# Epsilon added by GpSimd, indices and places without conversions, and a new order of VectorE's small steps

## What is computed

```
x = x + attn_a(layernorm(x));  x = x + ffn(layernorm(x))
x = x + attn_b(layernorm(x));  x = x + ffn(layernorm(x))

layernorm(x) = (x - mean) / sqrt(var + 1e-5)
ffn:  logits = tgt @ Wr.T + br;  top_v, top_i = top_k(logits, 2);  top_w = softmax(top_v)
      each token goes through its two experts (128 -> 512 relu -> 128), weighted by top_w,
      then gamma * layernorm(tgt + tgt2) + beta
```

## Time and profile before

| what | value |
|---|---|
| median of 3 runs | 945.51 us (942.33 to 946.16) |
| the profiled execution, its own time | 949.54 us |
| its span in the profile | 947.7 us |
| TensorE matmuls busy | 791.4 us, 84% |
| VectorE busy | 630.8 us, 67% |
| ScalarE busy | 473.8 us, 50% |
| GpSimd busy | 434.3 us, 46% |
| second attention, roughly | 427 to 749 us |

### The profile page before, as it was taken

How to read it: one execution, slowest core, us unless ns; L and a number is a source line. 1 busy time by engine, 2 the same in 40 slices (tenths; PEclk the granted TensorE clock), 3 DMA queues, 4 the chain that set the end, 5 groups by cost and what they waited for, 6 DMA issues and landing times.

```text
span 947.7 us, 20829 instructions
## 1 busy us (share of the span) xinstructions
PE 791.4 (84%) x6270; PEld 565.3 (60%) x6270; DVE 630.8 (67%) x2348; ACT 473.8 (50%) x1130; POOL 434.3 (46%) x516
## 2 busy tenths in 40 slices
PE   3599989988898899934899998999998799999920
PEld 1356655655687799931455555555544488999920
DVE  3457777764466466644888997898895475666657
ACT  3356666654332233312377776776766432433424
POOL 3002444443466376541243664565322475666643
PEclk9999999996799999975699998999998899999965
DMA  7635554450567777723434534443420378777754
GB/s 198 142 88 122 133 125 121 121 120 28 159 203 222 210 228 240 224 78 105 129 109 132 142 104 123 122 131 108 132 88 27 119 213 251 236 225 240 223 161 123
DMA packets 111668, 142.28 MB, mean 150 GB/s; under 512 B 14912, under 2 KB 90560, under 8 KB 108992
## 3 DMA queue, kind: packets, MB, share of 16 engines
q1 hardware_dynamic: 102480, 122.19, 47.2%
q0 software_dynamic: 9088, 18.89, 5.9%
HBM read 102.89 MB, written 36.66 MB: 147 GB/s over the span
## 4 chain that ended last, share of the span: by engine, by line
PE 55%; DVE 18%; issue 7%; DMA 7%; SPq 5%; ACT 5%; POOL 2%; DVEq 0%; POOLq 0%; ACTq 0%
PE attn L1466 13%; PE attn L740 6%; PE score L1457 6%; PE max L1457 6%; DVE mx L989 6%; PE max L706 5%; PE score L682 4%; PE misc L776 3%; PE misc L748 3%; DMA qst<-scr 2%; PE misc L806 2%; ACT prob L459 2%; PE attn L1446 2%; DMA qst<-mparts 2%; DVE stats L350 1%
## 5 line engine op out<-in xcount | busy, mean ns | idle before, releaser
L989 DVE TENSOR_REDUCE mx<-max 128x2 f32<-128x512 f32 x352 | 237.6, 682 | 83.9 <-PE max L706 77.8
L459 ACT ACTIVATE prob<-score 128x512 f32<-128x512 f32 x352 | 206.1, 602 | 118.0 <-PE score L682 115.3
L1542 POOL DMA_INDIRECT ys<-yt,idw x156 | 150.3, 964 | 113.3 <-DVE yt L1517 85.0
L1289 POOL DMA_INDIRECT xs<-row,index x128 | 127.7, 998 | 149.6 <-ACT prob L459 132.9
L1466 PE MATMUL attn<-wsl,prob 128*128 128x128 f32 x1248 | 157.4, 279 | 2.8 <-DVE prob L1530 2.1
L706 PE MATMUL max<-kst,qst 72*128 72x256 bf16 (+2 forms) x768 | 141.8, 275 | 20.1 <-DVE mx L989 13.3
L1466 PEld LDWEIGHTS attn<-wsl,prob 128*128 128x128 f32 x1248 | 149.0, 195 | 5.7 <-DVE prob L1530 3.7
L682 PE MATMUL score<-qst,kst 74*128 74x256 bf16 (+2 forms) x768 | 138.4, 270 | 3.7 <-DMA qst<-mparts 1.7
L1482 ACT ACTIVATE prob<-score,wsl 128x256 f32<-128x256 f32 x78 | 36.9, 473 | 189.8 <-PE score L1457 189.6
L740 PE MATMUL attn<-prob,vaug 128*32 128x256 f32 (+1 forms) x1536 | 119.8, 385 | 1.0 <-ACT prob L459 0.6
L368 POOL TENSOR_TENSOR rstd<-rstd,halfm 128x2 f32<-128x2 f32 (+1 forms) x65 | 51.5, 793 | 144.6 <-DVE rstd L361 143.6
(11 more groups left out here) (147 smaller groups left out, 1159.2 us busy)
## 6 DMA issues: line engine op xcount, KB each, us to landing
wsl<-in_wall SPq DMA_DIRECT2D x78, 578.0 KB, 4.3
scr<-parts SPq DMA_DIRECT2D x32, 384.0 KB, 3.0
qst<-scr SPq DMA_DIRECT2D x64, 192.0 KB
xt<-xs SPq DMA_DIRECT2D x78, 132.0 KB
kst<-scr SPq DMA_DIRECT2D x16, 576.0 KB
row<-row SPq DMA_DIRECT2D x32, 128.0 KB, 3.9
yg<-ys SPq DMA_DIRECT2D x32, 128.0 KB, 2.9
kst<-scr SPq DMA_DIRECT2D x16, 192.0 KB
```

Source lines behind the costliest of these rows:

```text
L459: nc.scalar.activation(prob[:, g % 2, k, :], pS[(g * NB + k) % 2][:, :], ACT.Exp)\
L989: nc.vector.tensor_reduce(mx[:, sl[4], a:a + 2 * n - 1:2], pM[(g * NB + k) % 2][:, :].rearrange("p (h w) -> p h w", h=n), axis=AX.X, op=AL ...
L1289: nc.gpsimd.indirect_dma_start(out=xs, out_offset=bass.IndirectOffsetOnAxis(ap=index[:, slot, c, k:k + 1], axis=0), in_=row[:, slot, c, k, ...
L1542: nc.gpsimd.indirect_dma_start(out=ys, out_offset=bass.IndirectOffsetOnAxis(ap=idw[:, k, c, 0:1].bitcast(U32), axis=0), in_=yt[:, k, c, :] ...
```

## The change

GpSimd adds epsilon itself, ahead of the power; `dve_eps` is gone. The one-hot compares the uint32 indices with the numbers of the experts directly. The sum over experts becomes a maximum (all terms but one are zero, and none is negative) and writes uint32. So `ixf` and `placed` with their conversions are gone, `choose` has five parts in place of six and `send_to` four in place of five. With the parts left, the order of `step` on VectorE is written anew: in the second attention the t norm's statistics, its mean and variance, the places and its bias stand one to two banks later than before. The final norm of the last stage keeps its epsilon on VectorE.

```diff
--- before.py
+++ after.py
@@ -209,12 +209,10 @@
         lg = sb("lg", [P, RING, QC, E])
         mx8 = sb("mx8", [P, RING, QC, 8])
         ix8 = sb("ix8", [P, RING, QC, 8], U32)
-        ixf = sb("ixf", [P, QC, 2])
         oh = sb("oh", [P, QC, 2, E])
         ohb = sb("ohb", [P, RING, QC, E], BF16)
         place = sb("place", [P, QC, E])
         pick = sb("pick", [P, QC, 2, E])
-        placed = sb("placed", [P, QC, 2])
         index = sb("index", [P, RING, QC, 2], U32)
         run = sb("run", [P, E])
         dv = sb("dv", [P, RING, 3, QC])
@@ -271,12 +269,12 @@
             return sems[name]
 
         for name in """consts_in x_in proj_in weights_in consts_made geo_made filled vaug_zero wq_ps wq_made ones_set spare_in
-            c_sum c_add c_stats1 c_stats c_eps c_rstd c_bias c_norm c_gam c_bet c_x
+            c_add c_norm c_gam c_bet c_x
             n_stats1 n_stats n_eps n_rstd n_bias ln_ready lnT_ps lnT_sb qk_ps part1 less1 part2 less2 part3 v_ps v_sb
             max_ps max_read mxT_ps m_hi m_lo exp_ps exp_done av_done o_sb oT_ps rden_done on_done onT_ps onT_sb
             pr_ps x_ready t_stats1 t_stats t_eps t_rstd t_bias t_ready tT_ps tT_sb lg_ps lg_done mx8_done ix8_done
-            ixf_done diff e_done oh_done ohb_done den_done w0_done w1_done rank_ps place_done rank_read pick_done
-            placed_done index_done id_done chain chosen_made table_ps tiles_known pad_known pads_in xT_ps xT_sb idw_done h_ps h_act h_dve y_ps
+            diff e_done oh_done ohb_done den_done w0_done w1_done rank_ps place_done rank_read pick_done
+            index_done id_done chain chosen_made table_ps tiles_known pad_known pads_in xT_ps xT_sb idw_done h_ps h_act h_dve y_ps
             ysum_sb xf_done yt_sb out_w flags_set x_bet l_add l_stats1 l_stats l_eps l_rstd l_bias l_norm l_gam
             l_x""".split():
             s_(name)
@@ -355,14 +353,11 @@
                 ins = nc.vector.bn_aggr(mv[:, which, slot, c, :], stats[:, which, c, :])
             return ins
 
-        def dve_eps(dve, which, pre, v, slot):
-
-            dve.wait_ge(pre + "_stats", v)
-            nc.vector.tensor_scalar(rstd[:, which, slot, :, 0], mv[:, which, slot, :, 1], EPS, None, ALU.add)\
+        def pool_rstd(pool, which, pre, v, slot):
+
+            pool.wait_ge(pre + "_stats", v, apart=True)
+            nc.gpsimd.tensor_scalar(rstd[:, which, slot, :, 0], mv[:, which, slot, :, 1], EPS, None, ALU.add)\
                 .then_inc(s_(pre + "_eps"), 1)
-
-        def pool_rstd(pool, which, pre, v, slot):
-
             pool.wait_ge(pre + "_eps", v)
             half = halfm[:, which, :] if isinstance(which, slice) else halfm[:, 0, :]
             nc.gpsimd.tensor_tensor(rstd[:, which, slot, :, 1], rstd[:, which, slot, :, 0], half, ALU.pow)\
@@ -1016,8 +1011,6 @@
                         for w in range(which.start, which.stop):
                             ins = dve_mean_var(w, slot)
                         ins.then_inc(s_("n_stats"), 1)
-                    elif i == 2:
-                        dve_eps(dve, which, "n", v, slot)
                     elif NORM in on_:
                         dve_bias(dve, LN, "n", v, slot)
 
@@ -1063,10 +1056,8 @@
                                                 ALU.subtract).then_inc(s_("diff"), 1)
                     elif i == 3:
                         dve.wait_ge("ix8_done", v)
-                        nc.vector.tensor_copy(ixf[:, :, :], ix8[:, slot, :, 0:2]).then_inc(s_("ixf_done"), 1)
-                    elif i == 4:
-                        dve.wait_ge("ixf_done", v)
-                        nc.vector.tensor_tensor(oh[:, :, :, :], ixf[:, :, :].unsqueeze(3).to_broadcast([P, QC, 2, E]),
+                        nc.vector.tensor_tensor(oh[:, :, :, :],
+                                                ix8[:, slot, :, 0:2].unsqueeze(3).to_broadcast([P, QC, 2, E]),
                                                 iota8.unsqueeze(1).unsqueeze(1).to_broadcast([P, QC, 2, E]),
                                                 ALU.is_equal).then_inc(s_("oh_done"), 1)
                     else:
@@ -1105,11 +1096,8 @@
                                                 dv[:, slot, 1, :], ALU.mult).then_inc(s_("w1_done"), 1)
                     elif i == 3:
                         dve.wait_ge("pick_done", v)
-                        nc.vector.tensor_reduce(placed[:, :, :], pick[:, :, :, :], axis=AX.X, op=ALU.add)\
-                            .then_inc(s_("placed_done"), 1)
-                    else:
-                        dve.wait_ge("placed_done", v)
-                        nc.vector.tensor_copy(index[:, slot, :, :], placed[:, :, :]).then_inc(s_("index_done"), 1)
+                        nc.vector.tensor_reduce(index[:, slot, :, :], pick[:, :, :, :], axis=AX.X, op=ALU.max)\
+                            .then_inc(s_("index_done"), 1)
 
                 def shift(i):
 
@@ -1142,7 +1130,7 @@
 
                 def t_stats(i):
 
-                    if TNS in on_ and i < 3:
+                    if TNS in on_ and i < 2:
                         v, slot = V[TNS], sl[TNS]
                         if i == 0:
                             dve.wait_ge("x_ready", v, apart=True)
@@ -1150,9 +1138,7 @@
                         elif i == 1:
                             dve.wait_ge("t_stats1", v, apart=True)
                             dve_mean_var(TN, slot).then_inc(s_("t_stats"), 1)
-                        else:
-                            dve_eps(dve, TN, "t", v, slot)
-                    if RTE in on_ and i == 3:
+                    if RTE in on_ and i == 2:
                         dve_bias(dve, TN, "t", V[RTE], sl[RTE])
 
                 if isinstance(s, int) and s == TABLE_AT:
@@ -1162,7 +1148,7 @@
                 if li == 0:
                     maxima(0, 0)
                     shift(0)
-                    t_stats(3)
+                    t_stats(2)
                     more(1, 1)
                     shift(1)
                     norms(-1)
@@ -1170,49 +1156,44 @@
                     norms(1)
                     normed(0)
                     more(1, 1)
-                    norms(2)
                     maxima(0, 2)
                     maxima(1, 0)
                     choose(0)
-                    norms(3)
+                    norms(2)
                     maxima(1, 1)
                     choose(1)
                     choose(2)
                     more(1, 0)
+                    maxima(1, 2)
                     choose(3)
-                    maxima(1, 2)
                     choose(4)
-                    choose(5)
                     more(1, 0)
                     x_ready()
                     t_stats(0)
                     t_stats(1)
-                    t_stats(2)
                     more(1, 1)
-                    for i in range(5):
+                    for i in range(4):
                         send_to(i)
                 else:
                     maxima(0, 0)
                     shift(0)
                     shift(1)
+                    maxima(0, 1)
                     t_stats(0)
-                    maxima(0, 1)
+                    maxima(0, 2)
                     t_stats(1)
+                    maxima(0, 3)
                     send_to(0)
-                    maxima(0, 2)
+                    maxima(1, 0)
+                    send_to(1)
+                    more(1)
+                    maxima(1, 1)
+                    send_to(2)
                     t_stats(2)
-                    send_to(1)
-                    maxima(0, 3)
-                    send_to(2)
-                    maxima(1, 0)
+                    maxima(1, 2)
                     send_to(3)
-                    more(1)
-                    t_stats(3)
-                    maxima(1, 1)
-                    send_to(4)
                     more(2)
                     norms(-1)
-                    maxima(1, 2)
                     maxima(1, 3)
                     maxima(2, 0)
                     norms(0)
@@ -1224,13 +1205,11 @@
                     choose(2)
                     normed(0)
                     maxima(2, 3)
+                    maxima(3, 0)
                     choose(3)
+                    maxima(3, 1)
+                    choose(4)
                     norms(2)
-                    maxima(3, 0)
-                    choose(4)
-                    maxima(3, 1)
-                    choose(5)
-                    norms(3)
                     if early(li, s, on_):
                         normalise(dve, nc.vector, b[0], sl[0])
                         scale(dve, nc.vector, b[0], sl[0])
```

## The result

| | before | changed |
|---|---|---|
| median of 20 executions each | 947.36 us (942.33 to 952.93) | 954.98 us (945.81 to 970.1) |
| the profiled execution | 949.54 us, span 947.7 | 953.14 us, span 951.3 |
| granted clock in it | 0.923 | 0.930 |

The changed kernel is slower: ratio 1.0055 (95% interval 1.0029 to 1.008), 5.2 us. Ratios, here and in the table of the experiments, leave out disturbed executions (of the changed kernel seven, 960 us and up), while medians hold them; the two here lie 7.6 us apart. The sum of the prediction was +9.5 us, its range 945 to 967.

The account below looks back on a forecast made before the run. No engine is full, so single waits decide, with VectorE's order from bank (0,0) to `run` on the second attention's loop. 9.2 + 3.0 - 2.4 - 0.3 = +9.5 us, median 955.0, range 945 to 967.

Parts of the forecast that it names:

- The three arcs: Second attention, one step's loop: queries and keys to third send 9.61, to VectorE's bias, back 5.97; period 17.67 us.
- Places wait for two more banks: Second attention, VectorE: banks (0,3) and (1,0) go ahead of `run`; 0.73 us in six steps, 0.91 in five, sum 9.2.
- Epsilon on GpSimd: Second attention: n norm's epsilon stands between send and power, 0.37 us in each of steps 8 to 15, 3.0 together.
- First attention, -2.4 and -0.3: No index conversion ahead of bank (0,0): 0.2 us sooner in 12 steps, -2.4; bank (0,1) sooner in step 7, -0.3.
- Step 12: Second attention, a turn of the loop: TensorE restarts at half clock and is itself late, so only 0.2 us.
- Part 1 and 2: Second attention: places waiting for two more banks, 9.2 us, and the n norm's epsilon on GpSimd, 3.0 us.
- VectorE is the bound and `run` late is made up: Rival, second attention: TensorE's wait for `run` is absorbed and VectorE's saved work counts; -8.7 us, 937; chance 0.11.
- Half absorbed: Rival: denominator free, GpSimd's epsilon hidden, some delay of queries and keys caught up; +2 us, 947.5; chance 0.14.
- The clock: Rival, second attention: TensorE's new 1.3 us idle lowers its clock in five of eight steps; +10 on top, 965; chance 0.10.

Follow-up runs that it names:

- the old order: The changed kernel with only VectorE's order in the second attention put back as before; ratio 0.9889 to the kernel before, median 936.84 us.
- one bank earlier: The changed kernel with `send_to(1)`, the step that adds to `run`, moved ahead of bank (1,0); ratio 0.9974 to the kernel before, median 948.17 us.
- one bank more: The changed kernel with one more 128x512 maximum of a spare tile on VectorE ahead of `run`; ratio 1.0249 to the kernel before, median 971.94 us.

## Why the prediction was right, and where it was off

- **The three arcs through `run`, the third send and the bias.** Right. They close at 18.65 after the change, and the step moved with each arc when it alone was changed: `run` by one bank, the epsilon by plus or minus one. With `run` brought forward the step follows it only so far: in the old order without the epsilon TensorE is itself the later one, by 0.28.
- **Places wait for two more banks, 0.73 in the ordinary steps, 0.91 in step 8 and the late ones.** Measured 0.68, and 0.80 to 0.97 in steps 16 to 18; step 19, for which I had the same 0.91, gave 0.22. Of the terms the epsilon's 0.57, freed, was read rightly. The denominator was to be held up to 0.20 by GpSimd's send, and I took 0.10. It is 0.25 long and ends at 547.55 as the send does (546.46 + 1.09), but the next instruction starts 0.17 after it, where in the old order without a send beside it that is 0.09 (611.12 to 611.21): 0.08. The Trainium skill (SBUF — State Buffer, "SBUF: two separate sides") has the pair locked for the whole instruction; the trace agrees, the denominator ends as the send does. But the 0.20 that I had for that rule ran from its start to the send's end, and the denominator's own 0.17 lies in that time; its length grew by 0.08 too.
- **Epsilon on GpSimd, 0.37.** Measured 0.33 from start to start (0.31 on the arc), with its handoff at 0.09 (559.25 to 559.34) where I had taken 0.18 from the power's handoff to L403. The Trainium skill (GPSIMD Engine Reference, section 3.1) keeps elementwise work on VectorE as the rule; the 0.34 that a step gains when this add goes back there agrees.
- **First attention, -2.4 and -0.3.** The mechanism and its 0.21 are in the rows to the hundredth; steps 9 to 17 gave -2.5, where 0.21 each is 1.9; step 11 alone gave 0.55, for which I had no reason. The further -2.3 of the profiled pair (step 18, last step, beginning) is within what those parts differ by between profiles of the same code.
- **Step 12, "I take 0.2".** This step of the prediction failed. I read the half clock in the earlier trace rows and took TensorE to be late there for good. What stood there was VectorE, 2.40 us without an instruction, a cost of 4.4 us that belongs to the kernel before alone. Shifting VectorE's code takes it away, and the change shifts it. Steps 11 and 12 were +1.7 in my sum, all terms of Part 1 and 2 together, and came out at -2.3.
- **Its rivals.** That VectorE is the bound and `run` late is made up: refuted by the step and by one bank earlier. Half absorbed: refuted in the loop, where nothing is absorbed. The total, +5.2 by the ratio, lies nearer to its +2 than to my +9.5 all the same, but for another reason, the stand. The clock: it falls in step 8 of both profiled executions (2.75 us), in none of their other steps up to step 17, at idle times of 1.07 to 1.19 us, and in each step with one bank more. In the third of the executions that lie at 960 us and above, a long fall at the end comes on top by the one trace of them, 17 us, which was in no term of the sum; this rival was more alive than its 0.10.

The +3.6 us of the profiled pair is 11.0 for the loop, 2.75 for a fallen clock, -4.4 for the stand, -4.8 for the first attention (2.5 of it the change's for certain), -2.3 and +1.3 for the rest. The median came out on the forecast, 955.0, but against a median before that was 1.9 above the one shown, and with that third of the executions in it: the size was right by luck, the sign and the step by reasoning. In a steady step the new order costs 1.04 (17.61 to 18.65) and GpSimd's epsilon 0.34 (17.27 to 17.61); VectorE's epsilon out of `run`'s way, and with it the conversions, gives 0.40 back (17.67 to 17.27). The changed kernel in the old order is 1.1% faster than before, of which the missing stand is 0.46% (4.4 us).

Open: where 3 to 4 us of the gain of the old order come from, why step 8 loses its clock and the like steps after it don't, and why the DMA at the end comes late in some executions and not in others.

## What to carry to other kernels

Close the loop of a steady step before costing an edit: name the waits on it, check that the arcs add up to the period, and put every moved instruction on an arc or beside it. An instruction that only frees a shared buffer for another engine, as `run` does here, belongs as far forward as its inputs allow, even if the engine that runs it has work that looks more urgent. Where a step of a regular pipeline is out of line with its neighbours, find out why before taking it as a given: it may be a cost of the kernel before that an edit removes by moving code, and be mistaken for the edit's own gain.

## What the hardware showed that I had not expected

- VectorE stood 2.3 to 2.4 us at one turn of a hardware loop without waiting for any engine or data (`[2.40 <-issue]`), while a packet of the instruction queue was on its way. Whether it does depended on where the loop lies in its stream: 16 copies of [128x4] far ahead of it took it away. The price was 4.4 us, with the half clock that follows on TensorE.
- TensorE restarted at the lower clock (1.2 GHz) after idle times of 1.08 us in one step and not after 1.19 in the others of the same execution. With 1.67 to 1.78 us (one bank more) its first matmuls from step 9 on still ran at full clock (1.13), and it was at the lower one within 1.9 us of the restart (1.06 for L794 at 567.49), in each steady step.
- Waits of 1.86 to 2.19 us for a DMA began a long fall, waits of 1.61 and 1.62 us for the same DMA did not. Behind the one of 1.86 us, in the repeat of the changed kernel (961.2 us span), the granted clock was 0.62 and then 0.50 for two whole steps, with TensorE busy 22.38 of 24.45 us and 26.77 of 27.69. Being busy did not bring the clock back there. TensorE's timeline at its start:

```profile
690.07 0.39 PE L701 MATMUL max<-kst,qst 72*128 72x256 bf16 x2
692.33 0.38 PE L677 MATMUL score<-qst,kst 74*128 74x256 bf16 x2 [1.86 <-DMA qst<-mparts]
```

- A small add on GpSimd, [128x4], takes 0.24 us, and 0.09 more until the next instruction on the same engine that waits for it starts.
